# Mixture of experts in a two-layer tower: all ups of a sequence in one run, then all its downs

## The reference, cut to what matters

```python
def _L1_ffn_ref(x, Wg, bg, W1, b1, W2, b2):      # E, H, K = 8, 128, 2; D = 64
    gate_scores = x @ Wg + bg
    _, idx = jax.lax.top_k(gate_scores, K)
    mask = jax.nn.one_hot(idx, E, dtype=x.dtype).sum(axis=-2)
    h = jax.nn.gelu(jnp.einsum('td,edh->teh', xf, W1) + b1[None], approximate=False)
    y = jnp.einsum('teh,ehd->ted', h, W2) + b2[None]
    out = jnp.einsum('ted,te->td', y, mf)
...
h = h + _L1_ffn_ref(_layernorm(h, axis=-1), ...)
```

## Time and profile before

| what | value |
|---|---|
| median of 3 runs | 923.12 us |
| profiled execution, its own time | 922.11 us |
| its span, first to last instruction | 920.3 us |
| TensorE busy | 883.9 us (96%) |
| VectorE busy | 601.5 us (65%) |
| ScalarE busy | 576.7 us (63%) |
| GpSimd busy | 386.7 us (42%) |
| mixture, first up to last store's addition | about 619.5 to 918.2 us |

### The profile page before, as it was taken

The page is one execution under the profiler, slowest core; times in us unless marked ns, Lnnn a source line. Parts: engine busy times, 40 slices in busy tenths (PEclk is TensorE's granted clock), DMA queues, the critical chain, the costliest instruction groups (busy, mean ns, idle before and its releaser), DMA issues.

```text
span 920.3 us, 21834 instructions
## 1 busy us (share of the span) xinstructions
PE 883.9 (96%) x6184; PEld 627.8 (68%) x6198; DVE 601.5 (65%) x2605; ACT 576.7 (63%) x1196; POOL 386.7 (42%) x528
## 2 busy tenths in 40 slices
PE   4789999999999999989999999999999999999998
PEld 3666667666666666756667667667777777777775
DVE  5967777777878989977777777873343434344321
ACT  2346666666666666656666666676666666666664
POOL 1224444444348888834434444343333232323200
PEclk9989999999999999999999999999999999999999
DMA  4000000000002222200000000000000000000000
GB/s 105 2 2 1 1 0 0 0 0 0 2 1 59 69 74 70 76 1 1 1 0 0 0 0 1 1 1 7 19 11 17 11 17 11 17 11 17 12 18 18
DMA packets 18995, 15.13 MB, mean 16 GB/s; under 512 B 5762, under 2 KB 18946, under 8 KB 18946
## 3 DMA queue, kind: packets, MB, share of 16 engines
q1 hardware_dynamic: 18946, 14.52, 5.6%
HBM read 10.32 MB, written 4.19 MB: 16 GB/s over the span
## 4 chain that ended last, share of the span: by engine, by line
PE 83%; DVE 12%; issue 2%; ACT 1%; DMA 1%; DVEq 0%; POOL 0%; SPq 0%; ACTq 0%
PE bank L1259 13%; PE bank L1074 13%; PE bank L1239 7%; PE bank L1040 7%; PE bank L1240 6%; PE bank L987 5%; DVE nmax L752 5%; PE bank L1065 5%; PE bank L1066 5%; PE bank L1012 3%; PE bank L1151 3%; PE bank L1053 2%; PE bank L1029 2%; PE bank L1030 2%; PE bank L1019 1%
## 5 line engine op out<-in xcount | busy, mean ns | idle before, releaser
L752 DVE TENSOR_REDUCE nmax<-bank 128x1 fp32r<-128x512 f32 x256 | 170.4, 687 | 45.7 <-PE bank L1040 45.3
L373 POOL TENSOR_TENSOR XS<-XN,XS 128x252 fp32r<-128x252 f32 x128 | 97.8, 764 | 202.3 <-ACT XS L415 202.3
L355 POOL TENSOR_TENSOR rstd<-VE,half 128x4 f32<-128x4 f32 x128 | 129.4, 1011 | 107.8 <-DVE VE L672 107.7
L517 ACT ACTIVATE PT<-bank 128x512 f32<-128x512 f32 x256 | 145.9, 596 | 40.2 <-PE bank L1066 33.3
L367 POOL TENSOR_TENSOR XN<-XC,rstd 128x252 f32<-128x252 f32 x128 | 78.1, 610 | 182.4 <-PE bank L1074 182.3
L575 ACT ACTIVATE PT<-bank 128x512 f32<-128x512 f32 x256 | 132.5, 604 | 4.9 <-PE bank L1240 4.1
L488 ACT ACTIVATE OT<-bank 128x256 f32<-128x256 f32 x96 | 36.9, 384 | 152.3 <-PE bank L1074 102.2
L1074 PE MATMUL bank<-PT,XN 128*64 128x256 f32 x1024 | 124.6, 385 | 0.0
L1259 PE MATMUL bank<-PT,W 128*64 128x256 f32 x1024 | 124.4, 385 | 0.0
L1040 PE MATMUL bank<-X,QH 128*128 128x512 f32 x252 | 105.6, 420 | 7.1 <-DVE nmax L752 0.7
L1065 PE MATMUL bank<-QH,X 128*128 128x512 f32 x256 | 112.2, 438 | 0.0
(11 more groups left out here) (144 smaller groups left out, 1486.4 us busy)
## 6 DMA issues: line engine op xcount, KB each, us to landing
WR<-experts SPq DMA_DIRECT2D x64, 129.0 KB, 2.0
out<-H SPq DMA_DIRECT2D x32, 128.0 KB, 1.7
W<-pack SPq DMA_DIRECT2D x5, 252.5 KB, 4.1
W<-pack SPq DMA_DIRECT2D x1, 251.5 KB, 4.8
W<-pack SPq DMA_DIRECT2D x1, 243.0 KB, 5.4
tk<-tokens SPq DMA_DIRECT2D x1, 64.0 KB, 4.4
route_sb<-route SPq DMA_DIRECT2D x1, 0.2 KB
```

The source lines that it names most:

```text
L355: pl.tensor_tensor(rstd[:, par, :], VE[:, par, :], half[:, :], ALU.pow).then_inc(sigma_done, 1)
L517: sc_.activation(PT[:, par, kt, :], bank[4 + kt % 2][:, :], ACT.Exp, scale=SCALE).then_inc(s.e_ready, 1)
L752: v.tensor_reduce(nmax[:, par, t:t + 1], bank[first + t % 2][:, :], axis=AX, op=ALU.max, negate=True).then_inc(s.max_ready, 1)
```

## The change

On TensorE all eight ups of a sequence stand in a row, with the next sequence's gate behind the second, and all eight downs of the same sequence in a row behind the turn back; no down is carried over to the next sequence. On ScalarE the copy of the sums comes first in the body, then eight gelus, the masks, and only then the rounding (`high_on`) and X2.

```diff
             def ffn1(i, par, lane):
-                for e in range(4):
-                    gelu(i, e)
                 if not known(i) or i >= 1:
                     evac_o(f1, a1, bank[6 - par], i - 1, 1 - par)
-                high_on(f1, a1, None, 3, i + 3, 1 - par, (lane + 3) % 4)
-                for e in range(4, NEXP1):
+                for e in range(NEXP1):
                     gelu(i, e)
                 if has(i + 1):
                     masks(i + 1, 1 - par)
+                high_on(f1, a1, None, 3, i + 3, 1 - par, (lane + 3) % 4)
                 if has(i + 2):
                     evac_x(f1, i + 2, par)
...
             def ffn1(i, par):
-                for e in range(4):
+                for e in range(2):
                     up(i, par, e)
                 if has(i + 1):
                     gate_scores(i + 1, 1 - par)
-                if not known(i) or i >= 1:
-                    for e in range(4, NEXP1):
-                        down(i - 1, 1 - par, e)
-                for e in range(4, NEXP1):
+                for e in range(2, NEXP1):
                     up(i, par, e)
                 down_bias(i, par)
                 if has(i + 1):
                     turn_masks(i + 1, 1 - par)
                 if not known(i) or i >= 1:
                     turn_back(f1, a1, i - 1, 1 - par)
-                for e in range(4):
+                for e in range(NEXP1):
                     down(i, par, e)
...
             sweep(pe, ffn1)
-            for e in range(4, NEXP1):
-                down(NSEQ - 1, 1, e)
             turn_back(f1, a1, NSEQ - 1, 1)
```

## The result

| | before | after |
|---|---|---|
| median of 9 runs each | 922.99 us (922.04 to 924.87) | 918.01 us (916.41 to 920.67) |
| ratio to before, 95% interval | | 0.9943 (0.9932 to 0.9954) |
| profiled execution, its own time | 922.11 us | 918.59 us |
| its span | 920.3 us | 916.8 us |
| from the mixture's first up to the end | 300.8 us | 294.7 us |

The changed kernel is faster by 0.57% (0.46 to 0.68), 5.0 us between the medians; 916.6 had been forecast, with a range of 914.0 to 921.4. The mixture alone is 6.1 us shorter in the profiles, where 6.5 had been worked out. The last row of the table takes 2.6 us of it back in these two profiles: the mixture starts later, though nothing ahead of it was changed.

The account below looks back on a forecast made before the run. TensorE's row of matmuls was taken to bound the mixture. Gains of 8.7 us less 1.3 (masks) and 0.9 (gate's operand) gave 6.5: 915.6 us profiled, 916.6 as median, range 914.0 to 921.4.

Parts of the forecast that it names:

- The edges: TensorE in the mixture: joined downs and fewer changes of matmul kind save 0.26 a sequence, 31 x 0.26 = 8.1 us.
- The last term, the 0.66 of sequence 0: TensorE's wait of 0.66 at sequence 0's turn of the masks is covered by six ups behind the gate, not four.
- The gate's operand: TensorE's gate, two ups earlier, waits for ScalarE's X2: 0.03 late at 30 gates, 0.9 us lost, between 0 and 3.3.
- The bound from the nearest row: Least lead of a weight load, read from up 0's load and second matmul: 0.10, putting the gate 0.03 late.
- The masks: In the loop VectorE's masks come 3.58 after the gate, 0.06 late for TensorE: 22 x 0.06 = 1.3 us lost.
- GpSimd: Its run begins 6.25 after the first up, clear of VectorE's masks at 4.3; rival, they meet: 928.5 us, chance 0.07.

Follow-up runs that it names:

- The two-block run: Kernel before with only the gate moved behind the second up, downs 4 to 7 still in their own block: 927.63 us, ratio 1.0048.
- the second set: The changed kernel run once more, beside two versions with a shorter VectorE chain on one chip: 917.9 us, ratio 0.9929.

## Why the prediction was right

- *The edges.* 0.26 a sequence was forecast. Outside the loop 9.32 became 9.10, and 9.08 where X2 is no wait, which is 0.24; the 32 downs take 3.60, as worked out from the last block of before. The two-block run shows the edges directly. The last term, the 0.66 of sequence 0, is there: the changed kernel turns the masks of sequence 1 at 3.52 after the gate, without a wait.
- *The gate's operand.* The forecast was a gate 0.03 late. It starts on time (1.42 to 1.44 after the turn), but its four matmuls take 0.38 or 0.39 instead of 0.36. The price is the same, its place is one step later. The bound from the nearest row (0.10 of lead for a load) was measured as 0.11 where no lead is left. The Trainium skill's rule ("TensorE: Matmul & The Clock Gate", "The mechanism"), by which only loads on other rows overlap a matmul, does not hold here: taking the lead away costs 0.11. The same section also lets a load into "the background weight buffer" go ahead of matmuls under way, and the loads here fit that. One reading of the prediction is off: the matmul that starts with the gate's load in the kernel before (787.57) is the second of its up, over 80 rows and not 128; the rows still overlap.
- *The masks.* 3.58 after the gate was forecast, against 3.52 for TensorE; measured are 3.59 and 3.52. The step that was sized too small is its number: the first sequence of the loop waits 0.21 and not 0.06 (its masks start 3.39 after the gate, not 3.25), so the term is about 21 x 0.07 + 0.21 = 1.7 and not 1.3. In before that slower sequence was hidden by the downs.
- *GpSimd.* Forecast: its run begins 6.25 after the first up. Measured 6.40 (786.74 to 793.14), and the masks' instruction took 0.18. The run with ScalarE's old order shows what stood on it.
- *The sum.* 6.5 forecast for the mixture, 6.1 measured: 0.4 more for the masks. The median fell by 5.0. The rest, 1.1, I put down to the granted clock ahead of the mixture, which differs from execution to execution in all kernels. For the first set this is not shown, since the clocks of most of its executions of before are not on record. In the second set (924.06 and 917.9, a difference of 6.2) they are: executions at a mean granted clock of 0.996 have medians of 922.9 and 916.2, those at 0.994 of 924.1 and 918.1. At like clocks the change is worth 6.7 and 6.0, about what the mixture shows.

## What to carry to other kernels

Where one engine bounds a stage with its queue full, count the places where its work changes kind: here a block of 16 downs between ups cost 0.36 us beyond its matmuls, and joining two blocks saved that much in each sequence, of which the gate's new place took 0.15 back. Before work is taken out from between a request and its answer, add up the answer's chain on the other engines, because the work that leaves was also its cover; here two chains came out within 0.1 us of their cover, and one position of the gate to either side made the kernel over 10 us slower. What a third engine does at the moment of the answer belongs to that sum: order the work that wakes it behind the answer.

## What the runs showed of the hardware

The same VectorE instruction on a 128x32 tile took 0.18 us alone, 0.47 when it began 0.30 into a GpSimd subtraction of 0.73, and 0.72 when it began 0.04 into one of 0.72: both times it ended 0.04 behind GpSimd's. A gate whose weight load had no lead took 0.47 us where one with the usual lead took 0.36. In the hardware loop VectorE's chain from gate to masks is 0.32 longer than in the written-out sequences (3.25 against 2.93 to the masks' start), and 0.46 longer in the loop's first sequence. The granted clock differs between executions with the same instructions, in the embedding (0.93 and 0.97 from 12 to 62 us in the two profiles of the changed kernel) and where the second attention begins (1.00 and 0.83 from 400 to 410 us), and each time the start of all that follows moves by one to two and a half microseconds.
